# Loads split in the normalisation stage, half of a load stream moved from ACT's queue to POOL's, and doubled buffers in the last stage's eviction

## The reference

```python
x = hidden_states                              # (4, 2048, 4096) float32
xn = _layernorm(x, axis=-1)
# attention: 32 heads of 128, causal, ALiBi bias, softmax
qkv = xn @ w_attn + b_attn
scores = where(causal, einsum('bqhd,bkhd->bhqk', q, k)/128 + bias, -inf)
attn = einsum(softmax(scores), v) @ w_proj + b_proj
# masked dense layer
dots = softmax(xn @ centroids.T / 0.1)         # 64 clusters
hits = dots > 0.01
query_sel = any(hits, axis=1); cluster_sel = any(hits, axis=0)
row_sel = cluster_sel[assignments]
ffn = where(query_sel[:, None] & row_sel[None, :], xn @ weight.T + bias, 0)
return x + attn + ffn
```

## Time and profile before

| what | us |
|---|---|
| median of the timed runs (2 runs, 7122.45 to 7191.5) | 7156.97 |
| the profiled execution | 6863.03 |
| its slowest core, first to last instruction | 6861.5 |
| its fastest core | 6792.0 |

### The profile page before, as it was taken

How to read it: one execution, slowest core, us unless ns; L and a number is a source line. 1 busy time by engine, 2 the same in 40 slices (tenths; PEclk the granted TensorE clock), 3 DMA queues, 4 the chain that set the end, 5 groups by cost and what they waited for, 6 DMA issues and landing times.

```text
span 6861.5 us, 80017 instructions; the slowest of 8 cores (6792.0 to 6861.5 us)
## 1 busy us (share of the span) xinstructions
PE 4557.6 (66%) x20715; PEld 1964.0 (29%) x20715; DVE 1846.2 (27%) x4169; ACT 1444.8 (21%) x2628; POOL 1377.1 (20%) x2365
## 2 busy tenths in 40 slices
PE   2217988889898886565666566355555556777766
PEld 1103433333333332122112112122222223333322
DVE  4421111111111111433433333355433322222222
ACT  4320000000000000222222222133444422222222
POOL 0022222222222221232232222000000012222222
PEclk9999999999999998677777777566655568888888
DMA  3332222222222224443444444211111134444343
GB/s 131 118 95 77 79 81 77 81 81 79 79 78 81 76 82 127 125 144 117 133 141 124 123 138 131 98 47 47 38 47 47 47 110 137 140 135 136 123 133 122
DMA packets 388507, 687.07 MB, mean 100 GB/s; under 512 B 59361, under 2 KB 226273, under 8 KB 381921
## 3 DMA queue, kind: packets, MB, share of 16 engines
q1 hardware_dynamic: 263410, 346.56, 16.2%
q0 software_dynamic: 87936, 268.54, 12.3%
q10 hardware_dynamic: 36720, 66.86, 3.1%
HBM read 606.22 MB, written 75.50 MB: 99 GB/s over the span
## 4 chain that ended last, share of the span: by engine, by line
PE 53%; DVE 15%; DMA 12%; ACT 9%; issue 7%; POOL 1%; SPq 1%; DVEq 1%; ACTq 1%; POOLq 0%
PE p2p L87 26%; PE qp L87 7%; PE f5b L87 7%; DMA d3x<-xT_all 6%; PE f5a L87 6%; ACT a4e L80 4%; DMA p2w<-w_attn 3%; DVE statc L80 2%; PE a4po L87 2%; PE d3pd L87 2%; PE a4pt L87 2%; DVE d3r L80 2%; DVE p2o L80 1%; ACT f5t L80 1%; DVE a4o L80 1%
## 5 line engine op out<-in xcount | busy, mean ns | idle before, releaser
L87 PE MATMUL p2p<-xn_fm,p2b 128*128 128x512 bf16 x8192 | 1893.0, 395 | 237.7 <-DVE p2b L80 140.6
L87 PEld LDWEIGHTS p2p<-xn_fm,p2b 128*128 128x128 bf16 x8192 | 821.7, 101 | 1308.7 <-issue 418.6
L87 PE MATMUL f5a<-ofm,f5pb 128*128 128x512 bf16 x2048 | 552.6, 394 | 297.0 <-DVE f5pb L80 297.0
L87 PE MATMUL qp<-xno,qb 128*128 128x512 bf16 x2048 | 481.8, 401 | 178.1 <-DVE qb L80 178.1
L87 PE MATMUL f5b<-xno,f5fb 128*128 128x512 bf16 x2048 | 543.3, 389 | 49.1 <-DVE f5fb L80 49.1
L80 DVE CAST p2b<-p2w 128x256 bf16<-128x256 f32 x512 | 160.4, 313 | 1485.3 <-PE p2p L87 1430.4
L87 PE MATMUL a4po<-a4a,a4e 128*128 128x129 bf16 x2304 | 332.4, 270 | 292.7 <-ACT a4e L80 278.7
L80 ACT ACTIVATE p2o<-p2p,battn 128x512 bf16<-128x512 f32 x128 | 87.9, 687 | 2056.0 <-PE p2p L87 2046.9
L80 DVE CAST d3b<-d3x 128x512 bf16<-128x512 f32 x512 | 364.8, 712 | 501.4 <-DMA d3x<-xT_all 432.1
L87 PE MATMUL d3pd<-d3b,centbf 128*64 128x512 bf16 x512 | 279.9, 547 | 326.9 <-POOL d3q L80 232.6
L80 POOL CAST p2b<-p2w 128x256 bf16<-128x256 f32 x512 | 208.4, 407 | 1275.4 <-DMA p2w<-w_attn 1008.8
(11 more groups left out here) (114 smaller groups left out, 3789.1 us busy)
## 6 DMA issues: line engine op xcount, KB each, us to landing
d3x<-xT_all SPq DMA_DIRECT2D x257, 256.0 KB, 4.0
p2w<-w_attn SPq DMA_DIRECT2D x512, 128.0 KB, 2.3
p2w<-w_attn POOLq DMA_DIRECT2D x512, 128.0 KB, 2.4
f5f<-ffn_wT POOLq DMA_DIRECT2D x512, 128.0 KB, 2.9
f5p<-w_proj SPq DMA_DIRECT2D x512, 128.0 KB, 2.7
d3x<-xT_all ACTq DMA_DIRECT2D x255, 256.0 KB, 3.1
qw<-w_attn POOLq DMA_DIRECT2D x256, 128.0 KB, 2.8
qw<-w_attn SPq DMA_DIRECT2D x256, 128.0 KB, 2.9
```

Source lines behind the costliest of these rows:

```text
L87: return getattr(self.e, method)(*args, **kw)
```

## The change

Three places are edited.

- Stage 1: each half tile is loaded by two DMAs of 512 KB on the same queue instead of one of 1 MB. The waits and the queues stay; the readers wait for all four.
- Stage 3: slots 3 to 5 of `d3x` are loaded from POOL's queue instead of ACT's. The semaphores stay (`acq`).
- Stage 5: `t1` and `t2` get a second buffer each, chosen by the block's parity; ACT's `t1` waits for the `osb` operation of two blocks back (`t_free[tp]`) instead of everything of DVE; and PE's first matmul of a group no longer waits for DVE's last `osb`.

```diff
@@ stage 1
-                    SY.dma(sq[1 + s], xt[s][:, 0:2048], src[:, 0:2048],
-                           waits=[(AC.ch, x_done[s]), (DV.ch, xd_dv[s])])
-                    PO.dma(posq[6 + s], xt[s][:, 2048:4096], src[:, 2048:4096],
-                           waits=[(AC.ch, x_done[s]), (DV.ch, xd_dv[s])])
+                    wts = [(AC.ch, x_done[s]), (DV.ch, xd_dv[s])]
+                    SY.dma(sq[1 + s], xt[s][:, 0:1024], src[:, 0:1024],
+                           waits=wts)
+                    SY.dma(sq[1 + s], xt[s][:, 1024:2048], src[:, 1024:2048])
+                    PO.dma(posq[6 + s], xt[s][:, 2048:3072], src[:, 2048:3072],
+                           waits=wts)
+                    PO.dma(posq[6 + s], xt[s][:, 3072:4096], src[:, 3072:4096])
@@ stage 3
                                 xqe, xch = ((SY, dsq[s]) if s < 3
-                                            else (AC, acq[s - 3]))
+                                            else (PO, acq[s - 3]))
@@ stage 5 (t1 and t2 become lists of two tiles, t_free = [0, 0])
                                         waits=([wp_done[s],
                                                 (AC.ch, ev_ac),
-                                                (DV.ch, ev_dv),
                                                 (sq[6], ofm_m)]
...
+                                tp = (2 * sub + rc) % 2
                                 ev_ac = AC.op(
-                                    "activation", t1[:],
+                                    "activation", t1[tp][:],
                                     ps_a[2 * sub + rc][:], AF.Identity,
                                     bias=bproj[:, fc:fc + 1], scale=1.0,
                                     waits=[(PE.ch, mm_done),
-                                           (DV.ch, DV.ch.n)])
+                                           (DV.ch, t_free[tp])])
                                 ev_ac = AC.op(
-                                    "activation", t2[:],
+                                    "activation", t2[tp][:],
...
-                                ev_dv = DV.op(
-                                    "tensor_tensor", osb[so][:], t1[:], t3[:],
+                                t_free[tp] = ev_dv = DV.op(
+                                    "tensor_tensor", osb[so][:], t1[tp][:],
+                                    t3[:],
                                     ALU.add, waits=[(gq[4 + so], o_done[so])])
```

More of the change, by code:

```diff
@@ L972, in emit_all @@
                         for s in range(2)]
-                    t1 = e5.enter_context(nc.sbuf_tensor("f5t1", [128, 512], F32))
-                    t2 = e5.enter_context(nc.sbuf_tensor("f5t2", [128, 512], F32))
+                    t1 = [e5.enter_context(
+                        nc.sbuf_tensor(f"f5t1{i}", [128, 512], F32))
+                        for i in range(2)]
+                    t2 = [e5.enter_context(
+                        nc.sbuf_tensor(f"f5t2{i}", [128, 512], F32))
+                        for i in range(2)]
                     t3 = e5.enter_context(nc.sbuf_tensor("f5t3", [128, 512], F32))
@@ L991, in emit_all @@
                     o_done = [0, 0]
+                    t_free = [0, 0]
                     ev_ac = 0
@@ L1063, in emit_all @@
                                 ev_dv = DV.op(
-                                    "tensor_tensor", t3[:], t2[:],
+                                    "tensor_tensor", t3[:], t2[tp][:],
                                     qselb[:, rc * 512:(rc + 1) * 512],
@@ L1068, in emit_all @@
                                 x_done[so] = DV.op(
-                                    "tensor_tensor", t1[:], t1[:], xres[so][:],
+                                    "tensor_tensor", t1[tp][:], t1[tp][:],
+                                    xres[so][:],
                                     ALU.add, waits=[(xq, xq.n)])
-                                ev_dv = DV.op(
-                                    "tensor_tensor", osb[so][:], t1[:], t3[:],
+                                t_free[tp] = ev_dv = DV.op(
+                                    "tensor_tensor", osb[so][:], t1[tp][:],
+                                    t3[:],
                                     ALU.add, waits=[(gq[4 + so], o_done[so])])
```

## The result

The changed kernel is slower: it took 1.0354 times as long as the kernel before, with a 95% interval of 1.0304 to 1.0404. On 6863 us that is +243 us (209 to 277). The profiled execution took 7156.85 us against 6863.03. The two timed runs shown ahead of the prediction were taken with part of the chip at a lower granted clock, as some executions of every kernel here are, and the executions without it, the only ones compared from here on, took 6845 to 6893 us (kernel before) and 7092 to 7157 us (changed kernel), so that my 7319 us stood on a base about 290 us too high.

A forecast was written before the change was run, and what follows sets the result against it. No engine was taken to bound the kernel; stage 3's score phase was read as a chain of latencies. The sum +234 - 72 + 0 = +162 us on 7157 gave 7319 us, +2.3%, range 7165 to 7440.

The forecast's parts named there:

- part 1: Stage 3, moved `d3x` loads: a round of six slots takes 11.3 us instead of 8.6, +234 us (+114 to +370).
- Two full landings in series in each round: Stage 3, POOL's queue: square 3 waits for load 3, load 5 is issued behind it, square 5 waits for load 5.
- One sign that I named: Stage 3: PE's wait for POOL's squares, 232.6 us before, would more than double.
- I take 3.2: Stage 3: assumed landing in us of a 256 KB `d3x` load on POOL's queue, counted twice a round.
- 4.9 + L3 + L5: Stage 3 round: 4.9 us of squares, issues and small waits, plus two landings, forecast as 2 x 3.2, in all 11.3.
- the landings are short: Rival, stage 3: landings under 3.1 us; with 2.8 the cost is 162 us, the time 7247 (+1.3%); chance 0.23.
- Part 2: Stage 5, doubled buffers: 2.4 us a block instead of 4.16, a 0.8 stall, turns of 12.9, -72 us (-59 to -85).
- Part 3: Stage 1, split loads: taken as 0, since bytes and queue stay; bounds -10 and +4 us.
- A: Rival, stage 3: the moved load is hidden anyway, rounds keep 8.6 us, only stage 5 counts: 7085 us; chance 0.10.
- above 3.6: Sign, stage 3: landings in us of POOL's loads beyond this would make the forecast wrong and point to B.
- B: Rival, stage 3: DVE's casts keep POOL from preparing loads, which land later; +307 (7392 us) or +452 (7537); chance 0.20.
- 7157 + 162: Whole kernel: base from the timed runs, 294 us above the profiled execution, plus the three parts' sum, giving 7319 us.

The follow-up runs named there:

- the four orders (0, 1, 2 and 4 steps): Kernel before with `d3x` slots 3 to 5 on POOL's queue, issued 0, 1, 2 or 4 steps ahead: score phases 65.0, 61.7, 49.4, 37.8 us.
- s3_alone: Kernel before with only the moved loads (slots 3 to 5 of `d3x` from POOL's queue): 7184.87 us, one execution, 5.0% slower.
- sp_small: Kernel before with slots 3 to 5 on POOL's queue and SP's loads cut to 128 of 512 columns after the first group: phases of 59.8 us.
- pool_ahead1: Kernel before with slots 3 to 5 loaded from POOL's queue, each issued one step ahead: 7125.80 us, one execution, 61.7 us a phase.
- pool_ahead2: Kernel before with slots 3 to 5 loaded from POOL's queue, each issued two steps ahead: 6932.97 us, one execution, 49.4 us a phase.
- pool_ahead: Kernel before with slots 3 to 5 loaded from POOL's queue, each issued four steps ahead: 0.9843 of before (0.9801 to 0.9886).
- act_ahead: Kernel before with slots 3 to 5 kept on ACT's queue but issued four steps ahead: 6635, 6648, 6652 us, about 0.973 of before.

## Why the prediction was right and wrong

Two steps failed: the base on which the time was put, and the size of one landing. The base alone put the time outside the range.

**The mechanism of part 1 held.** "Two full landings in series in each round" is what POOL's timeline shows and what the four orders (0, 1, 2 and 4 steps) confirm. The direction, slower by over 2%, followed. One sign that I named failed: PE's wait for POOL's squares did not double (232.6 to 256.7 us); most of the new wait is put down to ACT's square of load 4.

**The term that was mis-sized is the landing: "I take 3.2".** The page's row for the changed kernel gives exactly that:

```profile
d3x<-xT_all POOLq DMA_DIRECT2D x255, 256.0 KB, 3.2
```

But this is a median over three slots, of which two land in 3.1 and one in 4.3, and the two landings of a chain are one of each: 7.4 us instead of 6.4. The rest of my round stands, 4.9 + L3 + L5, in each kernel:

| kernel | L3 + L5 | round by 4.9 + L3 + L5 | measured round |
|---|---|---|---|
| changed | 4.32 + 3.14 | 12.4 | 12.4 |
| s3_alone | 4.20 + 3.12 | 12.2 | 12.2 |
| sp_small | 3.15 + 3.09 | 11.1 | 11.2 |
| pool_ahead1 (4.35 in place of 4.9, as the issue of load 4 falls into a wait) | 4.30 + 2.97 | 11.6 | 11.6 |

One us more a round is 85 us over 85.3 rounds; with the pauses before the phases, 11 us longer in all, this is the difference between my +234 and the +329 of stage 3. I had used ACT's median, measured with the traffic of the old round. The argument under "the landings are short", that SP's loads will have landed by then, was right for loads 4 and 5 and wrong for load 3: I asked how many loads share the DMA engines on average, and not what else is released by the event that releases this one.

**Part 2** was right in its mechanism and its parts: 2.39 us a block (2.4 forecast), a stall of 0.69 before the last `f5o` (0.8), turns of 12.9 (12.9), 71 us by itself (72). In the changed kernel 62 of them are seen. The missing 9 are inside the scatter of the stages; I have no run that finds them elsewhere.

**Part 3.** "I take 0": measured +5 to +7 us in the stage, just above my bound of +4. The second issue (0.54 us a tile) is on the path, as that bound assumed; what the rest of the 0.8 to 1.1 us a tile is was not tried apart.

**Rivals.** A (hidden anyway) is excluded by `s3_alone`. Short landings: excluded, as loads 3 and 5 took 4.3 and 3.1 and their mean is 3.7. By my own sign, "above 3.6", that is B's region, and B's lower half begins at +307 in stage 3; but its reason is wrong: `sp_small` takes the burst away, leaves every cast, and the late landing is gone. The rule of the Trainium skill that stood behind B (SBUF — State Buffer, the "DVE blocks DMA" trap) is thus not what made these loads late; `sp_small`'s 3.15 leaves it at most a few tenths. The shortest landing of these loads is 2.9 us from POOL's queue in the changed kernel and 2.5 from ACT's before; whether the casts or POOL's issue make that difference was not tried.

**The time.** The step that failed is "7157 + 162": 7319 us and the range of 7165 to 7440 stood on the median of the two timed runs. I had seen that they were 294 us above the profiled execution, took the difference to lie outside these chains, and carried it into the number all the same. The kernel before took 6845 to 6893 us, so the base was some 290 us too high, and the changed kernel took 7092 to 7157 us, below the range. The sum made on the profiled execution, 7025, is low by 94 us against the median of 7119: stage 3 cost 95 more than forecast, stage 5 gained 10 less, stage 1 cost 7, and stage 2 happened to be 15 shorter. The two errors partly cancel: 7319 is 200 us above that median, not 290.

## What to carry to other kernels

In an in-order queue, a load issued right ahead of its own reader can put its full landing into the chain of that queue: here two of three did. Before a load is moved to another engine's queue, write that queue's order down and count the landings in series. In this kernel the loads did best in a queue without readers (30.7 us a phase), and next best several steps ahead of their step (32.5 to 37.8), although they landed later there. And when a chain is priced with a latency, ask which other transfers the same event releases: the median of the queue hides the one transfer that meets the burst.

## What the runs showed of the hardware

- A 256 KB load from POOL's queue lands in a median of 3.1 us when it overlaps one other load of the stream (loads 4 and 5 of the changed kernel), in 4.2 to 4.3 when three others leave at the same moment (load 3), and in 5.5 when it overlaps five, four of them already out at its issue (load 5 of `pool_ahead2`). With SP's three shrunk to 64 KB load 3 took 3.15. In `pool_ahead` as many overlap, but they leave spread over the round, and the medians are 3.6 to 4.1.
- POOL's squares and DVE's casts slow each other. In the kernel before a cast takes 0.43 us alone or when it starts first, and mostly about 1.08 when a square is already running; a square takes 1.04 to 1.05 alone and up to 1.30 when a cast is already running.
- `act_ahead` and `pool_ahead` differ in the queue only, by 5 us a phase; how much of it are POOL's longer issues (0.55 against 0.33 us) and how much this interference is left open, as it wasn't tried apart.
- Two loads of 512 KB on one queue are not faster than one of 1 MB: from POOL's first issue to the last landing they took 6.1 us instead of 5.6, and the tiles that wait for them came 0.8 to 1.1 us later each.
